# A third PSUM bank for the transformed columns of the first pass, tile statistics moved behind the modes in another bank, and ScalarE's loop written out

## The reference

```python
# layer 0: group norm over pairs of channels, spectral convolution on 20 x 20 modes
x = x + _L0_conv_ref(_gn(x), L0_conv_weights1)
# layer 1: group norm, Sobel magnitude
x = x + _L1_conv_ref(_gn(x))

def _L0_conv_ref(x, weights1):
    x_ht = dht_2d(x)                                   # Hartley transform, divided by its norm
    out_modes = compl_mul2d(x_ht[:, :, :M1, :M2], weights1)   # mixes 64 -> 64 channels, per mode
    out_ht = zeros.at[:, :, :M1, :M2].set(out_modes)
    return idht_2d(out_ht)

def dht_2d(x):
    f = fftn(x, axes=(2, 3)); ff = fftn(x[..., ::-1, ::-1], axes=(2, 3))
    result = f.real - ff.imag
    return result / sqrt(sum(result * result))

def _depthwise_sobel(x):
    return jnp.sqrt(gx * gx + gy * gy + EPS)
```

## Time and profile before

| what | value |
|---|---|
| median of 3 runs (lowest, highest) | 2347.14 us (2346.33, 2347.58) |
| the profiled execution: its time, its span | 2346.94 us, 2345.1 us |
| PE busy over the span | 2212.0 us (94%) |
| ACT, DVE, POOL busy over the span | 1946.7 us (83%), 1759.6 us (75%), 1602.0 us (68%) |
| first pass | about 23.7 to 702 us |
| mixing | about 702 to 889 us |
| second pass | from about 889 us |
| DMA over the span | 180 GB/s, data queue 62.7% of the 16 engines' time |

### The profile page before, as it was taken

How to read it: one execution, slowest core, us unless ns; L and a number is a source line. 1 busy time by engine, 2 the same in 40 slices (tenths; PEclk the granted TensorE clock), 3 DMA queues, 4 the chain that set the end, 5 groups by cost and what they waited for, 6 DMA issues and landing times.

```text
span 2345.1 us, 60985 instructions
## 1 busy us (share of the span) xinstructions
PE 2212.0 (94%) x21204; PEld 1627.6 (69%) x21204; DVE 1759.6 (75%) x2670; ACT 1946.7 (83%) x3634; POOL 1602.0 (68%) x923
## 2 busy tenths in 40 slices
PE   5999999999992969999999999999999999999998
PEld 4878887888872956666666666666666666666665
DVE  4888888888872156877886887886787787787777
ACT  5888888888871128899898999998989989989998
POOL 4766666666661127777776777777777777777776
PEclk9999999999995568999999999999999999999999
DMA  7777777777787024666666666666666666666665
GB/s 208 206 199 201 199 201 206 197 205 202 200 201 151 2 73 123 186 187 181 188 183 180 187 180 191 182 186 181 180 180 191 188 184 183 182 187 180 197 188 163
DMA packets 808888, 421.40 MB, mean 180 GB/s; under 512 B 20912, under 2 KB 807344, under 8 KB 807472
## 3 DMA queue, kind: packets, MB, share of 16 engines
q1 hardware_dynamic: 808624, 417.86, 62.7%
HBM read 283.56 MB, written 134.22 MB: 178 GB/s over the span
## 4 chain that ended last, share of the span: by engine, by line
PE 61%; issue 1%; DVE 0%; ACT 0%; POOLq 0%; POOL 0%; DVEq 0%; ACTq 0%
PE g_ps L1080 43%; PE y_ps L1072 10%; PE v_ps L1060 7%; PE v_ps L1048 1%; PE g_ps L1100 0%; ACT coef_t L1189 0%; DVE coef L1249 0%; DVE xbuf L1261 0%; DVE xbuf L1233 0%; POOLq L894 0%; POOL p_lo L1021 0%; ACT g_ps L1154 0%; DVE g_ps L1239 0%; PE y_ps L1100 0%; ACT v_sb L1141 0%
## 5 line engine op out<-in xcount | busy, mean ns | idle before, releaser
L1080 PE MATMUL g_ps<-p_hi,stencil 128*128 128x512 f32 x2048 | 854.8, 417 | 9.5 <-DVE xbuf L1261 7.0
L1021 POOL TENSOR_TENSOR p_lo<-pairs,p_hi 128x1032 fp32r<-128x1032 f32 x256 | 617.1, 2411 | 313.9 <-ACT p_hi L1135 313.9
L1080 PE MATMUL g_ps<-p_lo,stencil 128*128 128x512 f32 x2048 | 820.6, 401 | 0.0
L1080 PEld LDWEIGHTS g_ps<-p_hi,stencil 128*128 128x128 f32 x2048 | 388.5, 190 | 289.5 <-POOL p_lo L1021 140.5
L1016 POOL TENSOR_TENSOR pairs<-xbuf 128x1032 f32<-128x1032 f32 x256 | 488.1, 1907 | 48.6 <-POOL p_lo L1021 30.1
L1239 DVE TENSOR_TENSOR g_ps<-gx,g_ps 128x512 f32<-128x512 f32 x512 | 351.3, 696 | 225.1 <-ACT g_ps L1154 217.0
L1261 DVE SCALAR_TENSOR_TENSOR xbuf<-xbuf,rows,g_ps 128x256 f32<-128x256 f32 x1024 | 436.2, 477 | 83.3 <-ACT g_ps L1160 61.4
L330 POOL TENSOR_TENSOR m_lo<-xbuf,m_hi 128x512 fp32r<-128x512 f32 x256 | 305.6, 1194 | 225.1 <-ACT m_hi L442 224.7
L1080 PEld LDWEIGHTS g_ps<-p_lo,stencil 128*128 128x128 f32 x2048 | 389.3, 190 | 81.8
L1160 ACT ACTIVATE g_ps<-g_ps,rows 128x256 f32<-128x256 f32 x1024 | 408.3, 445 | 27.4 <-DVE g_ps L1239 6.0
L523 DVE TENSOR_REDUCE rows<-square 128x1024 f32 (+1 forms) x256 | 311.0, 1215 | 116.5 <-ACT square L474 116.5
(11 more groups left out here) (125 smaller groups left out, 2328.3 us busy)
## 6 DMA issues: line engine op xcount, KB each, us to landing
xbuf<-x SPq DMA_DIRECT2D x256, 512.0 KB, 5.2
xbuf<-x SPq DMA_DIRECT2D x512, 256.0 KB, 3.1
out<-xbuf SPq DMA_DIRECT2D x512, 256.0 KB, 3.5
wmix<-weights SPq DMA_DIRECT2D x16, 800.0 KB, 18.9
second_sb<-second SPq DMA_DIRECT2D x1, 1230.0 KB, 8.3
mats_sb<-mats SPq DMA_DIRECT2D x1, 704.0 KB, 6.5
first_sb<-first SPq DMA_DIRECT2D x1, 32.0 KB, 5.5
```

The source lines that it names most:

```text
L1021: nc.gpsimd.tensor_tensor(p_lo[:, r % 2, :, 0:W + 1], pairs[:, r % 2, :, 0:W + 1], p_hi[:, r % 2, :, 0:W + 1].bitcast(FP32), ALU.subtract) ...
L1080: mm = nc.tensor.matmul(g_ps[h][:, axis], stencil[:, m, :], p[:, r % 2, 4 * h:4 * h + 4, o:o + W], start=n == 0, stop=n == len(todo) - 1)
```

## The change

Three things are changed together. The transformed columns rotate through three PSUM banks and no longer through two (`T_BANKS`): half n of the whole pass uses bank n modulo 3, and ACT's opening count on `first_out` is 3. The bank for this is that of `stat_ps`. The 32 columns of the statistics move to the end of `r_ps[1]`. So that PE and ACT don't meet in this bank, `stats` of a tile is now issued where the next use of the bank begins: in chunk 0, behind the wait on `modes_out`, ahead of the first piece of the second axis. The sums of tile i - 1, which stood behind chunk 5 of tile i, so stand in chunk 0 of tile i + 1. For the last tile it stands behind a wait of its own on the last copy of the modes. Since the bank number of an eviction now depends on the tile, ACT's loop over the tiles is written out. DVE, POOL and SP have the same instructions in the same order as before.

```diff
+T_BANKS = 3
...
-        t_ps = [ps(ctx, f"t_ps{g}", [128, HALF, PITCH]) for g in range(2)]
+        t_ps = [ps(ctx, f"t_ps{g}", [128, HALF, PITCH]) for g in range(T_BANKS)]
...
-        stat_ps = ps(ctx, "stat_ps", [128, 2, TILES])
+
+        stat_ps = r_ps[1][:, 480:512].rearrange("p (a t) -> p a t", a=2)
...
                 if k == 0:
-                    pe.wait_ge(first_out, (i + 1) * HALVES + 2)
+                    pe.wait_ge(first_out, (i + 1) * HALVES + T_BANKS)
                     pe.wait_ge(modes_out, i + 1)
+                    if i:
+                        stats(i - 1)
...
             def first_axis(i, k, g):
 
-                pe.wait_ge(first_out, i * HALVES + 2 * k + g + 1)
+                n = i * HALVES + 2 * k + g
+                pe.wait_ge(first_out, n + 1)
                 for p in range(HALF):
                     for c in range(2):
                         side = slice(64 * c, 64 * (c + 1))
-                        mm = nc.tensor.matmul(t_ps[g][side, p, :], xbuf[:, k % SLOTS, HALF * g + p, side], first[:],
+                        mm = nc.tensor.matmul(t_ps[n % T_BANKS][side, p, :], xbuf[:, k % SLOTS, HALF * g + p, side], first[:],
                                               start=True, stop=True)
...
-                    if k == 5 and not is_first(i):
-                        stats(i - 1)
...
                 second_axis(TILES - 1, 1, k)
+            pe.wait_ge(modes_out, TILES + 1)
             stats(TILES - 1)
...
-            act.sem_inc(first_out, 2)
+            act.sem_inc(first_out, T_BANKS)
...
-                                             t_ps[g][:, :, 0:NB], ACT.Copy).then_inc(first_out, 1)
+                                             t_ps[(i * HALVES + 2 * k + g) % T_BANKS][:, :, 0:NB], ACT.Copy)\
+                            .then_inc(first_out, 1)
...
-            over_tiles(act, tile)
+            for i in range(TILES):
+                tile(i, i % 2)
```

## The result

The changed kernel takes 2326.76 us (median of four runs, 2321.8 to 2328.83) against 2346.73 us for the kernel before beside it (2344.43 to 2347.58): a ratio of 0.9913, 95% interval 0.9901 to 0.9926. That is 20.0 us gained, where 27.3 were forecast (2319.8 us). The profiled execution took 2327.04 us, its span is 2325.2 us.

What follows compares the result with a forecast made beforehand. PE was taken to bound the first pass, losing time waiting for ACT's evictions. 30.4 - 2.8 - 0.3 = 27.3 us off 2346.94 gave 2319.6, with the median 0.2 above it 2319.8 us; range 2315 to 2332.

Steps and rivals of the forecast that it cites:

- What the third bank takes away: First pass: PE's 97 waits for ACT's eviction `tmodes` vanish, 90 x 0.31 + 7 x 0.36 = 30.4 us gross gain.
- the restart of the weight loads: At PE's bank wait: weight loads start only with the matmul, explaining the gain beyond 26.1 us idle, up to 30.4.
- What is late next: First pass, behind the pair: `m_lo` comes in time, slack 0.72 us, or 0.18 without second axis; PE stays the bound.
- The rival on `m_lo`: Chunks without second axis: `mirror` waits for `m_lo`, 7.2 us of gain lost, 2327 us; returned wait's chance 0.14.
- the slack of 0.18: Chunks without second axis: PE needs `m_lo` 4.10 us after `high`, POOL ends it after 3.92; thin, not used up.
- This rival's worse case: Returned wait: half of the other chunks lose their gain too, 2334 us; returned wait's chance 0.14.
- The statistics: Moved to chunk 0, they wait for ACT's copies about 0.2 us in 14 tiles, 2.8 us; last tile loses 0.3.
- no loss by themselves: The same four statistics records, about 0.43 us, move from chunk 5 to the next tile's chunk 0 without gain or loss.
- At the end of the pass nothing came through: Last statistics wait some 1.05 us for the last copies; costed at nothing, as mixing waits on the weights' transfer.
- ACT written out: ACT's loop over tiles: removed register arithmetic fell in time ACT had over, so no gain was taken.
- stops for instructions: ACT, first pass: one 5.9 us stop per tile leaving the loop, 14 x 5.9 = 83 us, 2403 us; chance 0.05.
- lower clock in the first pass: PE's granted clock falling to half for even 55 us would take the whole gain; chance 0.01.

Runs made afterwards that it cites:

- statistics back: Changed kernel with the statistics issued again behind chunk 5, in the same columns of r_ps[1], without clearing the bank: 2323.98 us, ratio 0.9899 to the kernel before.
- the run that takes the edges apart: Changed kernel with VectorE's edge work split: products in chunk 2, reduction in chunk 3, addition in chunk 4; 2310.71 us, ratio 0.9837 to the kernel before.
- combined kernel: Changed kernel (three banks) with edges in three pieces, the waits ahead of `high` swapped and statistics behind chunk 5: 2305.45 us, ratio 0.9819 to the kernel before.
- two banks (from 321.40): Changed kernel with T_BANKS = 2, its moved statistics and written-out ACT loop kept: 2363.34 us, ratio 1.0061 to the kernel before.

## Why the prediction was right in direction and over a third too large

**"What the third bank takes away": right, and sized too small.** All 97 waits are gone. The pair of halves without a wait takes 1.91 us (335.29 to 337.20), not the 2.09 that I took from chunk 6. That chunk follows the statistics, and its pair held a wait on the bank too small to show as idle time: in the run with the statistics back, where no such wait can be, the pair at the same place takes 1.91 (335.07 to 336.98). So a wait cost 2.40 - 1.91 = 0.49 us, not 0.31. The reason that the forecast gave for the part beyond the idle time, the restart of the weight loads, does not hold. Without a wait a half takes 1.91 / 2 = 0.96 us, but a half of 32 records is shown as 1.15 long, to its modelled end: 0.19 us of the wait hide there. The half behind the wait takes 301.37 - 300.38 = 0.99 us, so that the restart is worth 0.03. Idle time, hidden part and restart are 0.27 + 0.19 + 0.03 = 0.49. Per tile the six waits and the hidden one gave about 3.1 us.

**"What is late next": this is the step that failed.** It looked at `m_lo`, at ACT's sum of work and at DMA, and asked nothing of VectorE, which had 82.86 of 100 us. A mean of 83% hides a chunk in which VectorE carries the edges besides the squares and products. In a chunk of 5.31 us that fitted; in one of 4.81 it doesn't, once POOL's `m_lo`, which moved with ACT's `high`, starts ahead of the addition and holds it for 1.2 us. The price is 5.92 - 4.81 = 1.11 us in each of the 13 tiles that wait, 14.4 us; the run that takes the edges apart gave 14.6 back in the first pass and 16.05 in all. The rival on `m_lo` was true in chunk 7, which has no second axis: `mirror` of half 1 starts at 343.26, 1.29 us after half 0 at 341.97, and not 1.06. The `m_lo` that it needs ended at 343.12 (341.92 + 1.20, the slack of 0.18 was used up), and `prod` by 342.70. With the step behind it the chunk gained 0.18 us instead of 0.48, so 0.30 a tile. It shows as no idle time of PE's matmuls, and PE's share counts it as work. This rival's worse case was also added up wrong: half of the other 75 chunks at 0.31 are 11.6 us, which gives 2339 and not 2334.

**"The statistics": the wait was right, "no loss by themselves" was not.** From the pair to the statistics it takes 305.53 - 303.33 = 2.20 us. A product of 128 rows, as the statistics and `mirror` have, starts 2.02 us after the pair where it waits for nothing (chunk 7, 339.95 to 341.97), so the wait is 0.18, where 0.2 was forecast: 2.5 us over 14 tiles. PE's rows show no idle time for it; the weight loads show 3.2 us in 14, with no releaser named. But the four records cost more in their new place. In chunk 0 the way from the pair to `mirror` is 3.55 us (303.33 to 306.88) instead of 2.71 without statistics (chunk 3, 319.62 to 322.33), 0.84 more, 0.66 without the wait. In chunk 5 they had cost 5.76 - 0.49 - 4.94 = 0.33. So the move costs 0.33 a tile besides the wait, about 5 us, which the forecast had put at nothing. Why they are dearer there is open. At the end of the pass nothing came through, as forecast. The mixing's weights are issued earlier than the row that I read the earlier trace rows shows: that row lay in the middle of a group of 16 which begins at 678.04 in the kernel before and at 658.50 after.

**"ACT written out" as nothing: wrong for two banks.** It costs 5.6 us there, all of it by the order of two waits. With three banks it is nearly off PE's path: only chunk 7, where `m_lo` is late, is shorter with the waits swapped (4.36 us in the combined kernel, 4.42 and 4.41 in the runs without the swap), about 1 us over the pass. The rivals of stops for instructions and of a lower clock in the first pass didn't come: no gap of 2 us, and a granted clock of 1.00.

**The sum, as measured.** These are the distances in us from the start of one chunk to the start of the next, on PE, in one tile of each kernel:

| chunk | 0 | 1 | 2 | 3 | 4 | 5 | 6 | 7 | tile |
|---|---|---|---|---|---|---|---|---|---|
| before (from 314.17) | 5.29 | 6.19 | 4.93 | 5.30 | 5.29 | 5.76 | 4.83 | 4.61 | 42.20 |
| after (from 303.33) | 5.65 | 5.71 | 4.93 | 4.81 | 5.92 | 4.94 | 4.66 | 4.43 | 41.05 |
| edges in three pieces (from 298.06) | 5.67 | 5.72 | 4.92 | 4.82 | 4.81 | 4.93 | 4.67 | 4.42 | 39.96 |
| two banks (from 321.40) | 6.04 | 6.25 | 4.93 | 5.37 | 5.33 | 5.47 | 5.20 | 4.66 | 43.25 |
| statistics back (from 303.21) | 5.22 | 5.71 | 4.93 | 4.81 | 5.92 | 5.27 | 4.68 | 4.41 | 40.95 |
| all together (from 297.73) | 5.20 | 5.72 | 4.92 | 4.82 | 4.81 | 5.27 | 4.68 | 4.36 | 39.78 |

A tile gained 3.1 us from the bank and lost 1.11 to `prod`, 0.30 to `m_lo`, 0.18 to the copies and 0.33 to the statistics' new place, which leaves 1.18; 1.15 were measured. Over the pass the first tile gave 2.3 us (38.19 less 35.93), tiles 1 and 2 gave 4.1 (tile 1 has no statistics yet, tile 2 no wait on `prod`), tiles 3 to 14 gave 13.1, the last tile 2.3 and the end of the pass 0.5. PE began at 22.68 us before and at 22.76 after, which takes 0.1 off. Together these are the 22.2 us.

The total fell inside the range because errors offset each other, which is luck. The waits gave 15 x 3.1 us and 7 x 0.53 in the first tile (2.02 us to `mirror`, not 2.55), about 50 in all and not 30.4. Against these 20 us more stood 14.4 for `prod`, about 6 for `m_lo` with the first tile's share of 1.4, and 5 for the statistics' place, none of which the sum had.

## What to carry to other kernels

When a wait on the critical engine goes, ask of every other engine how much it does in its fullest chunk, not on average: an engine at 83% was late in one chunk of eight, and moving one addition, or spreading the side work over three chunks, gave 16 us more, beside the 20 of the change itself. Take the price of a wait from the distance of two starts where no wait can be, since idle times from modelled ends leave part of it out. Before small differences between kernels are read, compare the stretches that the edit doesn't touch: here eight instructions that do nothing were worth 7 us.

## What the runs showed that was not expected

- An addition of 128 numbers on VectorE took 0.29 us where it started ahead of GpSimd's `m_lo` and 1.21 to 1.32 us where it started 0.02 to 0.13 us behind it; two reductions with one input took 1.27 us together beside it, no longer each than the one ahead of it (0.69).
- The order of two waits ahead of one activation was worth 0.06 us each time in the written-out loop: 0.43 us from product to activation with the late wait given first, 0.49 with it given last, 5.6 us of 2349 in the whole.
- A semaphore wait with 0.27 us of idle time cost PE 0.49 us from start to start. 0.19 of the rest lie under the modelled end of the half ahead of it.
- Eight instructions more at the start of VectorE's program halved VectorE's stops in the second pass, from four to two of about 2.6 us each, and the granted clock behind the first stayed at 1.00, where it had been 0.83.
